# Scoring for the row maxima half a head group further ahead, six transfers of K and Q pieces a group, and a new prologue order, in a three-layer decoder kernel

## The chip, the cores and the metric

The kernel runs on one core of one Trainium2 chip. The metric is the device time of one launch in microseconds. Engines are named as in the profile: PE (matmuls), PEld (its weight loads), DVE, ACT, POOL, and SP, which here only issues DMAs.

## What is computed

Four sequences (B = 4) of 512 tokens of width 256 pass three layers, each with a residual and a LayerNorm behind it. Cut to what matters:

```python
# 1: recurrence with a gate, then an MLP
x_norm = layernorm(x) * g1 + b1
c_r, c_i = chunked_eigenstate(sigmoid(log_decay), frequency, x_norm @ w_in.T)   # 64 modes, chunks of 64
x1 = x + sigmoid(x_norm @ w_gate.T + b_gate) * (mix(c_r, c_i) @ w_out.T)
x = layernorm(x + x1 + silu(layernorm(x1) @ w_mlp1.T + b) @ w_mlp2.T + b2)
# 2: causal attention, 16 heads of 16, K and V from a second input
Q, K, V = x @ wq.T + bq, ctx @ wk.T + bk, ctx @ wv.T + bv
x = layernorm(x + softmax(causal(Q @ K.T / 4)) @ V @ wo.T + bo)
# 3: 48 experts, each takes its 64 best tokens; scatter-add of the weighted results
x = layernorm(x + experts(x))
```

## The kernel before

All five engines have a program of their own, written out by hand; they meet only in semaphores, and each engine takes its instructions strictly in the order of its own list. PSUM has eight banks of 512 float32.

**First layer** (to about 204 us). The batches are overlapped: while the MLP of batch b runs (`expand`, L1442, and `shrink`, L1451), the recurrence of batch b+1 goes through DVE and POOL. At the very start there is nothing to overlap. DVE builds the phases of the rotation first (14 chained instructions, L852 to L858, for the sine and for the cosine), and only then `ln_in(0)`: statistics (L824, L828), the root on POOL (L648, L650), the normalization (L837). ACT makes sine, cosine and then copies the transposed tokens out of PSUM with gain and bias (`turned_1`, L1207). PE transposes (L1397), projects (`project`, L1413 and L1420), mixes (L1430); for the second batch it takes `turn`, `turn_2(0)`, `project(1)`, in that order, and then the loop starts with `expand(0)`.

**Attention** (to about 530 us). The 16 heads of a batch go in four groups of four. For float32 accuracy K and Q are each split into three bfloat16 pieces. A score is contracted over 96 rows, six blocks of 16: K's pieces stand in them in the order 0, 1, 2, 0, 1, 0 and Q's in the order 0, 0, 0, 1, 1, 2. Three further rows (99 in all) carry minus the row maximum in Q, in three pieces, against ones in K. The pieces are computed feature by feature, stored to DRAM (`pieces`, L523 and L525) and fetched back per group into the right partitions (`group_in`, L537): 12 transfers of 16 partitions x 4 heads x 512 tokens, 64 KB, in runs of 1 KB.

For every group there are two passes over the scores:

- the **score pass** (`scores`, L1563 adds the causal mask, L1567 the product) writes query-major scores into two PSUM banks in turn, 11 banks a group, and DVE takes each bank's row maxima (`maxima`, L991). When all 11 are there, DVE negates and splits them (`negate`, L1002 to L1009), PE transposes them into the two spare banks (`minus_max`, L1579), and ACT copies them into Q's three extra rows (L1279);
- the **shifted pass** (`shifted`, L1597) computes key-major scores that already have the maximum subtracted, ACT takes the exponentials (L1292), POOL masks the diagonal (L711), and PE multiplies with V (`values`, L1610).

A group has four slots (b, g, j), one for each tile j of 128 keys. Lists called `PREPARE` (K, Q, V of the next batch), `ENTER` and `FINISH` (the output projection, LayerNorm and router logits of the batch that is done) say which further steps go into which slot; each engine works through the three step lists of a slot in order, between its shares of the score pass. The score pass of the *next* group (`then`) is spread over the slots: slot 0 has tiles 0 and 1 (three banks), slot 1 tile 2 (four), slot 2 tile 3 (four, all in the middle share), slot 3 none. `negate` closes slot 2 on DVE and `minus_max` stands in slot 3 on PE and ACT. The steps and `minus_max` and `heads_out` share the two spare banks (`take`): a step waits until the one before it in its bank has been read.

SP's list in a batch (`relay`) is: wait for and store K's and Q's pieces (`split_out`), fetch group 0 of the next batch, fetch the tokens, fetch groups 1 to 3, each behind the shifted pass that frees its place, fetch the context, store the outputs.

Before the first slot, the last MLP runs out; SP fetches all four groups; PE scores group 0, DVE takes its maxima; DVE normalizes the last batch; POOL computes that norm's root and *then* sets the ones in K (L723, four memsets), for which the first shifted pass waits.

**Experts** (to the end). After the top-64 selection on DVE (about 550 to 585 us) the weights of 24 pairs of experts stream through seven buffers.

## Time and profile before

| | us |
|---|---|
| median of three runs | 815.03 (811.88 to 816.0) |
| the profiled execution | 816.48 |
| its span | 814.7 |
| PE busy | 612.5 (75%) |
| DVE busy | 358.4 (44%) |
| ACT busy | 274.5 (34%) |
| POOL busy | 195.1 (24%) |

The page's second part divides the span into 40 slices of 20.4 us: PE's digits are 9 in slices 3 to 10 (the first layer), 7 and 8 through attention, and fall to 0 where the tokens are chosen; the DMA digit is 9 in the slices of the experts. The chain that ended last is PE 49%, DMA 16%, DVE 15%, issue 9%, ACT 7%. Busy shares are means over these unlike stages, so a reader should go to the stage: the PE's list in order of time shows for each instruction how long PE was idle ahead of it, and for whom.

### The profile page before, as it was taken

What the parts mean: (1) busy time and instruction counts of PE and PEld (TensorE: products, weight loads), DVE (VectorE), ACT (ScalarE), POOL (GpSimd) and SP (SyncE); (2) the same over time, 40 slices, a digit from 0 to 9 for tenths busy, and PEclk for the clock granted to TensorE, in tenths of its full rate; (3) what the DMA queues carried; (4) which work ended last, traced back from release to release, by engine and by line L of the source; (5) the groups of instructions that cost most, each with busy time, mean ns of one, the idle gap of its engine ahead of it and who ended that gap; (6) DMA issues with size and microseconds to landing.
All of it is one profiled execution on the core that took longest, in us unless ns stands there. A gap on an engine that the chain in (4) does not pass through costs nothing.

```text
span 814.7 us, 12126 instructions
## 1 busy us (share of the span) xinstructions
PE 612.5 (75%) x3942; PEld 351.0 (43%) x3942; DVE 358.4 (44%) x777; ACT 274.5 (34%) x458; POOL 195.1 (24%) x253
## 2 busy tenths in 40 slices
PE   3599999999467877787778788760089979789930
PEld 2458585847133445344534454340035535445520
DVE  3633533322564555455635564329823323223315
ACT  2141514141025463546354636510033322223304
POOL 1242221210051211021102111200032233335324
PEclk9899999999569899989998989965589999898965
DMA  6840000003410341134113334018159999994247
GB/s 229 299 162 1 0 0 0 25 27 108 138 40 1 113 140 45 40 116 135 38 46 114 109 114 179 1 53 338 84 176 372 408 387 326 315 378 88 35 98 231
DMA packets 53618, 112.25 MB, mean 138 GB/s; under 512 B 5920, under 2 KB 44496, under 8 KB 50512
## 3 DMA queue, kind: packets, MB, share of 16 engines
q1 hardware_dynamic: 48272, 105.06, 35.8%
q0 software_dynamic: 4608, 6.29, 4.1%
q10 hardware_dynamic: 704, 0.47, 0.2%
q8 instruction: 18, 0.29, 0.1%
q14 instruction: 16, 0.13, 0.1%
HBM read 91.88 MB, written 17.83 MB: 135 GB/s over the span
## 4 chain that ended last, share of the span: by engine, by line
PE 49%; DMA 16%; DVE 15%; issue 9%; ACT 7%; POOL 3%; SPq 1%; ACTq 0%; DVEq 0%; POOLq 0%
DMA sums<-row 9%; PE PS L1451 7%; PE PS L1442 7%; DMA sums<-wo_s,row 4%; DVE Mx L991 4%; PE PS L1730 4%; PE PS L1526 4%; PE PS L1610 3%; PE PS L1597 3%; PE PS L1567 3%; PE PS L1518 2%; PE PS L1413 2%; PE PS L1430 2%; PE PS L1563 2%; PE PS L1545 2%
## 5 line engine op out<-in xcount | busy, mean ns | idle before, releaser
L991 DVE TENSOR_REDUCE Mx<-PS 128x1 f32<-128x384 f32 (+3 forms) x176 | 107.3, 638 | 85.4 <-PE PS L1567 83.7
L1292 ACT ACTIVATE arena<-PS 128x512 f32<-128x512 f32 (+1 forms) x176 | 86.0, 565 | 87.6 <-PE PS L1597 87.6
L711 POOL TENSOR_SCALAR_AFFINE_SELECT arena<-arena 128x512 f32<-128x512 f32 x64 | 40.8, 638 | 217.9 <-ACT arena L1292 217.9
L1597 PE MATMUL PS<-arena 99*128 99x512 bf16 (+3 forms) x256 | 55.8, 307 | 26.3 <-ACT arena L1279 12.6
L1563 PE MATMUL PS<-causal,identb 128*128 128x128 bf16 (+2 forms) x176 | 45.8, 260 | 34.0 <-DVE Mx L991 24.7
L1567 PE MATMUL PS<-arena 96*128 96x128 bf16 (+3 forms) x256 | 68.1, 322 | 0.0
L1147 DVE TENSOR_TENSOR X<-PS,Y 128x512 f32<-128x512 f32 x48 | 31.4, 688 | 66.7 <-PE PS L1743 66.4
L1442 PE MATMUL PS<-arena 128*128 128x512 f32 x128 | 55.8, 593 | 1.6 <-issue 1.6
L1451 PE MATMUL PS<-arena 128*128 128x256 f32 x256 | 55.9, 379 | 0.0
L1359 ACT ACTIVATE X<-X 128x512 f32<-128x512 f32 x48 | 29.6, 632 | 71.3 <-DVE X L1147 68.1
L1610 PE MATMUL PS<-arena 128*32 128x128 f32 (+3 forms) x512 | 52.3, 481 | 1.0 <-POOL arena L711 0.9
L1451 PEld LDWEIGHTS PS<-arena 128*128 128x128 f32 x256 | 48.6, 190 | 6.6
L1563 PEld LDWEIGHTS PS<-causal,identb 128*128 128x128 bf16 x176 | 17.3, 98 | 72.5 <-DVE Mx L991 55.5
L1730 PE MATMUL PS<-ring_a,X 128*64 128x512 f32 x192 | 47.0, 635 | 0.5 <-ACT X L1348 0.5
L1597 PEld LDWEIGHTS PS<-arena 99*128 99x128 bf16 x256 | 21.2, 98 | 59.6 <-issue 17.5
L648 POOL TENSOR_SCALAR ve<-mv 128x4 f32<-128x4 f32 x16 | 3.7, 230 | 176.5 <-DVE mv L828 176.5
L1140 DVE COPY X<-PS 128x512 f32<-128x512 f32 x24 | 16.6, 692 | 66.1 <-PE PS L1730 66.1
L1730 PE MATMUL PS<-arena,X 128*64 128x512 f32 x192 | 44.6, 607 | 0.0
L1279 ACT ACTIVATE arena<-PS 3x1024 bf16<-3x1024 bf16 x32 | 30.8, 1009 | 40.3 <-PE PS L1579 40.2
L769 POOL DMA_INDIRECT sums<-row x16 | 25.6, 1597 | 64.6 <-issue 43.8
L1442 PEld LDWEIGHTS PS<-arena 128*128 128x128 f32 x128 | 24.2, 190 | 30.6 <-issue 30.0
L1207 ACT ACTIVATE arena<-PS,vec 128x512 f32<-128x512 f32 x16 | 11.4, 775 | 71.7 <-PE PS L1397 71.7
(183 smaller groups left out, 997.6 us busy)
## 6 DMA issues: line engine op xcount, KB each, us to landing
ring_a<-experts SPq DMA_DIRECT2D x12, 2048.0 KB, 10.2
arena<-experts SPq DMA_DIRECT2D x12, 2048.0 KB, 10.3
arena<-pieces SPq DMA_DIRECT2D x192, 64.0 KB, 2.3
ring_a<-experts SPq DMA_DIRECT2D x12, 512.0 KB, 4.8
arena<-experts SPq DMA_DIRECT2D x12, 512.0 KB, 7.4
pieces<-arena SPq DMA_DIRECT2D x4, 768.0 KB, 3.7
pieces<-ring_a SPq DMA_DIRECT2D x4, 768.0 KB, 3.7
X<-x SPq DMA_DIRECT2D x4, 512.0 KB, 3.6
```

Of the source, the lines that this page charges most:

```text
L711: pool.affine_select(out=pb[j % 2][:, :, 0:P], in_=pb[j % 2][:, :, 0:P], compare_op=ALU.is_ge, fill=0.0, base=0, pattern=[[0, GH], [1, P]] ...
L991: dve.tensor_reduce(Mx[:, g % 2, i, heads[0]:heads[-1] + 1], bank((g * NSH + u) % 2)[:, 0:len(heads) * w] .rearrange("p (h n) -> p h n", h ...
L1147: dve.tensor_tensor(hb[:, a * 512:(a + 1) * 512].rearrange("p (c n) -> p c n", c=8), bank(3 + a).rearrange("p (c n) -> p c n", c=8), b1_s[ ...
L1292: act.activation(pb[j % 2][:, heads[0]:heads[-1] + 1, 0:w], bank(2 + n % 3)[:, 0:len(heads) * w] .rearrange("p (h n) -> p h n", h=len(heads)),
L1442: mm = pe.matmul(bank(HIDDEN[m % 4]), wm1_s[:, k, m * P:(m + 1) * P], xT2[:, k, :], start=(k == 0), stop=(k == KT - 1))
L1451: mm = pe.matmul(PS[:, 6 * 512 + t * D:6 * 512 + (t + 1) * D], hid[:, m, t * P:(t + 1) * P], wm2_s[:, m, :], start=(m == 0), stop=(m == MT ...
L1526: mm = pe.matmul(o, w[:, k, :], xt[:, k, :], start=(k == 0), stop=(k == KT - 1))
L1563: pe.matmul(o[:, 0:len(heads) * w].rearrange("p (h n) -> p h n", h=len(heads)) [:, :, i * P:w], identb[:], wide(causal[:], len(heads)), st ...
L1567: mm = pe.matmul(o[:, a * w:(a + 1) * w], QTs[0:SK, g * GH + h, i * P:(i + 1) * P], KTs[0:SK, g * GH + h, 0:w], start=False, stop=True, sk ...
L1597: mm = pe.matmul(bank(2 + n % 3)[:, a * w:(a + 1) * w], KTs[0:SX, g * GH + h, j * P:(j + 1) * P], QTs[0:SX, g * GH + h, j * P:T], start=Tr ...
L1610: mm = pe.matmul(bank(6)[VW * h:VW * (h + 1), j * P:T], Vb[:, j, g * GH + h, :], pb[j % 2][:, h, 0:T - j * P], start=(j == 0), stop=(j == ...
L1730: mm = pe.matmul(bank(1 + n)[CAP * e:CAP * (e + 1), :], xgT[:, k, CAP * e:CAP * (e + 1)], w1_of[u][:, e, k, n * 512:(n + 1) * 512], start= ...
```

## The change

It does these things:

1. `SCORED`, `TILE_ORDER`, `AHEAD`: the tiles are scored in the order 3, 2, 0, 1. Slots 2 and 3 of group g score tiles 3 and 2 of group g+2; slot 0 of the next group scores tiles 0 and 1 of the same one, slot 1 none. `negate` moves to slot 0 on DVE, `minus_max` to slot 1 on PE and ACT.
2. `PREPARE`: K's projection moves from slot 1 to slot 0 of group 1, the query's input to slots 0 and 1, Q's last piece from slot 3 to slot 2; V's first half goes to the third list of its slot.
3. `group_in`: six transfers a group in place of twelve, of 3, 2 and 1 pieces' rows for K and the same for Q. The features inside a half of 128 are reordered on the host (`by_part`), so that the four heads of a group lie side by side: runs of 4 KB in place of 1 KB. A source is piece x feature x (head, token); where the same piece is wanted several times, its outermost step is zero.
4. The first shifted banks wait for the first of the two copies only.
5. Attention's start: the ones are set ahead of the last norm's root; after group 0, eight banks of group 1 are scored ahead of the first slot, and DVE takes the statistics of the last norm between the two.
6. The start of the kernel: DVE's statistics come ahead of the phases, its normalization ahead of them too; PE takes `project(1)` ahead of `turn_2(0)`.

```diff
-K_PIECES = (0, 1, 2, 0, 1, 0)
-Q_PIECES = (0, 0, 0, 1, 1, 2)
-NRD = 2 * NPR
+K_RUNS = ((0, 1, 3), (0, 1, 2), (0, 1, 1))
+Q_RUNS = ((0, 0, 3), (1, 0, 2), (2, 0, 1))
+NRD = len(K_RUNS) + len(Q_RUNS)
...
-TILES_OF = [(0, 1), (2,), (3,), ()]
-CUTS = [(2, 3), (2, 3), (0, 4), (0, 0)]
+TILE_ORDER = (3, 2, 0, 1)
+STARTS = [sum(len(SHARED_Q[t]) for t in TILE_ORDER[:n]) for n in range(TT)]
+SCORED = {i: list(zip([i] * NSH, range(start, NSH), SHARED_Q[i]))
+          for i, start in zip(TILE_ORDER, STARTS)}
+
+
+
+TILES_OF = [(0, 1), (), (3,), (2,)]
+AHEAD = (1, 1, 2, 2)
+CUTS = [(3, 3), (0, 0), (2, 3), (2, 3)]
 
 
 def _cut(tiles, cuts):
-    banks = [(i, n, heads) for i in tiles
-             for n, heads in enumerate(SHARED_Q[i], sum(len(q) for q in SHARED_Q[:i]))]
+    banks = [bank for i in tiles for bank in SCORED[i]]
     return banks[:cuts[0]], banks[cuts[0]:cuts[1]], banks[cuts[1]:]
 
 
-SCORED = [_cut(tiles, cuts) for tiles, cuts in zip(TILES_OF, CUTS)]
+SHARES = [_cut(tiles, cuts) for tiles, cuts in zip(TILES_OF, CUTS)]
 
 
 
 
 PREPARE = {
-    (1, 0): ([("query_in", 0)], [], [("query_in", 1)]),
-    (1, 1): ([("key", 0)], [("key", 1)], [("query", 0)]),
-    (1, 2): ([("split_k", 0)], [("query", 1)], []),
-    (1, 3): ([("split_q", 0)], [], []),
-    (2, 1): ([], [("value", 0)], []),
+    (1, 0): ([("key", 0)], [("key", 1)], [("query_in", 0)]),
+    (1, 1): ([("query_in", 1)], [("split_k", 0)], [("query", 0)]),
+    (1, 2): ([("query", 1)], [], [("split_q", 0)]),
+    (2, 1): ([], [], [("value", 0)]),
...
+                ahead = [None] + [(c, g + n) if g + n < NG else (c + 1, g + n - NG)
+                                  for n in (1, 2)]
+                for n in (1, 2):
+                    if last and g + n >= NG:
+                        ahead[n] = None
...
+                    do(c, g, j, prev, ahead[1], ahead[AHEAD[j]], *steps)
...
-                rows_g = slice(GH * HD * (g % 2), GH * HD * (g % 2) + GH * HD)
-                for n, (dst, order) in enumerate(((KTs, K_PIECES), (QTs, Q_PIECES))):
-                    for r, c in enumerate(order):
-                        sp.dma_start(dst[HD * r:HD * r + HD, heads, :],
-                                     pieces[n, c, g // 2, rows_g, :]
-                                     .rearrange("(h d) t -> d h t", d=HD)).then_inc(kq_in[g].s, 16)
+                at = GH * (g % 2)
+                for n, (dst, runs) in enumerate(((KTs, K_RUNS), (QTs, Q_RUNS))):
+                    first = 0
+                    for c, step, count in runs:
+                        part = pieces[n, c:c + (count if step else 1), g // 2]\
+                            .rearrange("c (d h) t -> c d h t", d=HD)[:, :, at:at + GH, :]\
+                            .rearrange("c d h t -> c d (h t)")
+                        if not step:
+                            part = part.to_broadcast([count, HD, GH * T])
+                        sp.dma_start(dst[first:first + HD * count, heads, :]
+                                     .rearrange("p h t -> p (h t)"), part).then_inc(kq_in[g].s, 16)
+                        first += HD * count
...
+            pool.wait_ge(vset, 2)
+            pool.wait_ge(m2.s, m2.now(B - 1, 1))
+            for g in range(NG):
+                pool.memset(KTs[SK:SX, GH * g:GH * g + GH, :], 1.0).then_inc(ones, 1)
+            pool.wait_ge(ones, NG)
...
+            dve.wait_ge(x_in.s, x_in.now(0, 1))
+            statistics(ln1, X, 0, 0, 0)
...
+            norm(ln1, rs1, X, lambda t: xn1[:, t, :], 0, 0, (xt1.s, xt1.before(0, 1)))
+            phase(0.0, rot[:, 0:C])
+            phase(0.25, rot[:, C:2 * C])
...
-            def dve_slot(b, g, j, prev, then, *steps):
-                shares = SCORED[j] if then is not None else ([], [], [])
-                maxima(then, shares[0])
+            def dve_slot(b, g, j, prev, then, scored, *steps):
+                shares = SHARES[j] if scored is not None else ([], [], [])
+                maxima(scored, shares[0])
                 if j == 0 and prev is not None:
                     divide(*prev)
                 dve_do(steps[0])
-                maxima(then, shares[1])
+                maxima(scored, shares[1])
                 dve_do(steps[1])
-                maxima(then, shares[2])
-                if j == 2 and then is not None:
+                maxima(scored, shares[2])
+                if j == 0 and then is not None:
...
+            for i in TILE_ORDER:
+                maxima((0, 0), SCORED[i])
             negate(0, 0)
-            ln_out_norm(B - 1)
+            dve.wait_ge(ln3.s, ln3.now(B - 1, 1))
+            statistics(ln3, X, (B - 1) * TT, B - 1, 1)
+            for i in TILE_ORDER[:2]:
+                maxima((0, 1), SCORED[i])
+            norm(ln3, rs3, X, lambda t: X[:, (B - 1) * TT + t, :], (B - 1) * TT, B - 1)
...
-                if j == TT - 1 and then is not None:
+                if j == 1 and then is not None:
...
             turn(ln1, xt1, xn1, 1, 4, (xe1.s, xe1.now(0, KT)))
+            project(1)
             turn_2(0)
-            project(1)
...
-                if j == 0:
-                    pe.wait_ge(nte.s, nte.now(b, 2 * g + 2))
                 for n, heads in enumerate(SHARED[j], FIRST[j]):
+                    if j == 0 and heads[0] % 2 == 0:
+                        pe.wait_ge(nte.s, nte.now(b, 2 * g + heads[0] // 2 + 1))
...
-            def pe_slot(b, g, j, prev, then, *steps):
-                shares = SCORED[j] if then is not None else ([], [], [])
+            def pe_slot(b, g, j, prev, then, scored, *steps):
+                shares = SHARES[j] if scored is not None else ([], [], [])
                 for n, _ in enumerate(shifted(b, g, j)):
                     of = len(SHARED[j])
-                    scores(then, shares[0][n * len(shares[0]) // of:
...
             minus_max(0, 0)
+            for i in TILE_ORDER[:2]:
+                scores((0, 1), SCORED[i])
...
+    by_part = lambda m: m.reshape(KT, 2 * GH, HD, -1).swapaxes(1, 2).reshape(m.shape)
...
+        "w_q": by_part(w("xattn_wq_w")).T,
+        "w_kv": np.concatenate([by_part(w("xattn_wk_w")), w("xattn_wv_w")]).T,
...
```

## Rows read from the trace of the kernel before

**Rows 1.** Busy time by stretch: each engine's busy us, PE clock, DMA share, GB/s.

```profile
209.70:530.00 320.30, 248.10 (x1812) 132.18 (x1812) 170.22 (x372) 151.30 (x264) 62.74 (x80) 0.90 0.26 84
...
611.00:652.00 41.00, 41.00 (x366) 20.67 (x362) 14.24 (x24) 13.43 (x25) 12.13 (x16) 1.00 1.01 390
```

**Rows 2.** PE's waits in attention, 250 to 530 us: total, times, longest.

```profile
PE PS L1563 <- DVE Mx L991: 23.4, 25, 3.6
PE PS L1597 <- ACT arena L1279: 11.3, 11, 1.3
```

**Rows 3.** PE in order of time: where each group's shifted pass starts.

```profile
329.33 0.60 PE L1597 MATMUL PS<-arena 99*128 99x512 bf16 x2
...
356.94 0.61 PE L1597 MATMUL PS<-arena 99*128 99x512 bf16 x2 [1.35 <-ACT arena L1279]
...
371.65 0.61 PE L1597 MATMUL PS<-arena 99*128 99x512 bf16 x2 [0.92 <-ACT arena L1279]
...
384.67 0.60 PE L1597 MATMUL PS<-arena 99*128 99x512 bf16 x2 [0.92 <-ACT arena L1279]
...
411.16 0.61 PE L1597 MATMUL PS<-arena 99*128 99x512 bf16 x2
```

**Rows 4.** PE in order of time, inside group 1.

```profile
340.42 1.88 PE L1526 MATMUL PS<-arena,wq_s 128*128 128x512 f32 x4
...
346.86 0.29 PE L1563 MATMUL PS<-causal,identb 128*128 128x128 bf16 x1 [3.57 <-DVE Mx L991]
...
347.97 3.62 PE L1526 MATMUL PS<-arena,wq_s 128*128 128x512 f32 x4
```

**Rows 5.** DVE in order of time: Q's last piece, then group 3.

```profile
354.97 1.23 DVE L966 TENSOR_TENSOR ring_a<-ring_a 128x1024 bf16<-128x1024 f32 x1 [1.13 <-ACT ring_a L1268]
...
372.74 1.47 DVE L991 TENSOR_REDUCE Mx<-PS 128x4 f32<-128x512 f32 x2 [3.77 <-PE PS L1567]
...
378.43 2.52 DVE L991 TENSOR_REDUCE Mx<-PS 128x1 f32<-128x512 f32 x4 [0.16 <-PE PS L1567]
...
381.73 0.18 DVE L1009 TENSOR_TENSOR nst<-Mr,nst 128x16 bf16<-128x16 f32 x1
```

**Rows 6.** ACT in order of time: the shift rows' copies in group 3.

```profile
382.69 1.93 ACT L1279 ACTIVATE arena<-PS 3x1024 bf16<-3x1024 bf16 x2 [0.72 <-PE PS L1579]
```

**Rows 7.** SP's issues: at attention's start, then in a batch.

```profile
202.16 22.79 SPq L537 DMA_DIRECT2D arena<-pieces  x48
...
356.22 0.37 SPq L525 DMA_DIRECT2D pieces<-ring_a  x1
360.11 5.48 SPq L537 DMA_DIRECT2D arena<-pieces  x12
```

**Rows 8.** DMA issues by line: count, KB each, median us to landing.

```profile
arena<-pieces SPq DMA_DIRECT2D x192, 64.0 KB, 2.3
```

**Rows 9.** All engines in order of time, attention's start.

```profile
219.62 1.86 PE L1579 MATMUL PS<-identb,nst 128*3 128x128 bf16 x16 [1.65 <-DVE nst L1009]
...
223.30 7.55 POOL L723 MEMSET arena<- 3x2048 bf16 x4 [0.32 <-POOL rstd L650]
...
230.90 1.04 PE L1597 MATMUL PS<-arena 99*128 99x512 bf16 x2 [9.41 <-POOL arena L723]
```

**Rows 10.** All engines in order of time, the kernel's start.

```profile
8.34 1.40 DVE L824 BATCH_NORM_STATS2 stats<-X 128x6 f32<-128x256 f32 x4 [0.17 <-DVE arena L858]
...
14.41 1.45 ACT L1207 ACTIVATE arena<-PS,vec 128x512 f32<-128x512 f32 x2 [5.96 <-PE PS L1397]
...
33.51 1.45 ACT L1207 ACTIVATE arena<-PS,vec 128x512 f32<-128x512 f32 x2 [6.76 <-PE PS L1397]
```

**Rows 11.** The chain that ended last, the kernel's start: start, us, what.

```profile
41.37 3.95 PE PS L1413 x8
45.32 3.45 PE PS L1420 x16
48.77 13.73 PE PS L1442 x32
```

32 lines of the change are left out of this document (10 added, 22 removed).

## The prediction

> **What bounds the kernel now.** I read the times by stage first, then PE's waits, then PE, DVE, ACT and the DMA queue in order of time over one batch of attention. Three stages follow each other. To 204 us the matmuls of the first block fill PE apart from its first 49 us; from 570 us the experts stream, with the DMA engines full [rows 1]; neither end is touched. Between them, from 209.7 to 530, lies attention, where PE is busy 248.1 of 320.3 us [rows 1], idle for over a fifth. Its two longest waits there are for row maxima of DVE, 23.4 us in 25 waits, and for the shift rows that ACT copies into Q, 11.3 us in 11 [rows 2]. A batch goes through four head groups, whose shifted pass starts at 329.33 (group 1), 356.94 (group 2), 371.65 (group 3), 384.67 (group 0 of the next batch) and 411.16 [rows 3]: 27.6 + 14.7 + 13.0 + 26.5 = 81.8 us. Group 3 does nothing but attention; group 1 also projects K and Q of the next batch, group 2 half of V, group 0 finishes the old batch.
>
> In group 3 the last maximum ends at 378.43 + 2.52 = 380.95. Then negation, transposes and copies follow, and the next shifted pass starts at 384.67 [rows 3, 5, 6]: 3.7 us in which DVE and most of PE hang on one chain. That chain is what the change takes off.
>
> **Part 1: scores half a group further ahead.** No instruction is added in a group; 11 banks of scores and 11 maxima stay. Slot 0 now holds three banks, slot 1 none, slots 2 and 3 four each. The plain group in its new order: DVE's first two maxima end at 1.1 + 1.4 = 2.5 us after the group's start [rows 3, 5], the third at 3.2, division 0.7 and negation 0.9 reach 4.8. PE finished the passes of slot 1 near 3.5, so it waits some 1.4 us in front of the transposes, a wait that the change adds, with the first value matmuls queued behind it. Transposes 0.7 and values 1.0 end at 6.6. Then come eight banks, bound by DVE: four of 0.63 [rows 5] and four of 0.56 (estimate from the same row, three quarters of the width and a fixed part) are 4.8, with 0.8 for the first fill and the last values. Sum 12.2 where it was 13.0. The shift chain is hidden under slots 1 to 3, but the maxima now bunch where PE has least else to do: **0.8 us a group**, not 3.7. Group 2 the same with its half of V: 14.0.
>
> Group 1: before, four banks stood behind DVE's last piece of K, a stall of 3.57 us, and the next Q projection then ran at the lower clock, 3.62 instead of 1.88 [rows 4]. Both go (K's pieces are prepared in slots 0 and 1, where no maxima are queued behind). Against that, ACT's second exponentials stand behind the K pieces, and the transposes' second bank waits for the query copy: 1.4 back. 27.6 - 3.6 - 1.7 - 0.8 + 1.4 = 22.9. The last piece of Q (1.23 us on DVE [rows 5]) is then done some 20.8 us into the group, against 26.9 before [rows 3, 5].
>
> Group 0: the transposes now stand between the two output projections and share their two spare PSUM banks. The first needs output 0 read by DVE (0.9), the second output needs both copies of ACT out of the bank, 1.93 us [rows 6]: +2.9. At its end the four further maxima and the normalization stand in front of the last values, and eat the 0.8 of the plain group and 0.2 more. 26.5 + 3.1 = 29.6. A batch: 22.9 + 14.0 + 12.2 + 29.6 = 78.7, **3.1 less, 9.3 in the three full batches**. In the last batch group 1 gains 0.8; group 2 scores only three banks and needs about 6.6 + 2.4 = 9.0 (4.0 less): -4.8. Bounds: my walk of the two loaded groups may be off by 2 us each; a batch gains from -1 (loses 1) to 6 us.
>
> **Part 2: prologue.** The statistics go ahead of the 14 phase steps on DVE. Before, the phase steps end and the statistics start at 8.34, and ACT evacuates the first transposes at 14.41 [rows 10]. Now the statistics start with the input, near 4.8 (estimate: the steps started near 4.9, each 0.23, and I assume the input no later), norm and root end near 9.6, the steps near 12.9, and ACT, whose order is unchanged, is held by the cosine to 13.2: -1.2. Projection 1 (3.95 + 3.45 us) stood behind the transposes of the second norm, from 41.37, though its input left ACT at 33.51 + 1.45 = 34.96 [rows 10, 11]. Placed ahead it ends near 41.3, the transposes and ACT's copy end at 44.1 where the hidden layer started at 48.77: -4.5 with the 1.2. PE is then busy without a break, so all of it should reach the end. Bounds -3 to -5.5.
>
> **Part 3: the ones and the priming.** The memsets, 7.55 us on POOL, end at 230.9, and PE waited 9.41 us for them [rows 9]. They move behind the MLP's last matmul at 202.2 and run beside the transfers of the first group: nothing is left of them; the root on POOL behind them is not late, since its statistics come after 217. What is late next: eight more banks of the second group are scored first, 8 x 0.63 = 5.0, and DVE's statistics, 2.0, stand ahead of their maxima. Scoring group 0 and its negation took from the landing at about 209.7 to the transposes at 219.62 [rows 8, 9], 9.9 us. The start therefore hangs on when the pieces land, which is part 4.
>
> **Part 4: six transfers a group.** Before, 48 issues take 22.79 us, 0.475 each, and one of 64 KB lands 2.3 us after its issue [rows 7, 8]: group 0 after 11 x 0.475 + 2.3 = 7.5. Now a group is 3, 2 and 1 rows of pieces, twice, in runs of 4 KB instead of 1 KB. No row shows such a transfer; every one of before has 16 or more rows as the outermost dimension of both sides, the new sources have 3 or 2 (the pieces). Lower bound: spread over all 16 engines, a group lands in 5 x 0.475 + 2.3 = 4.7 us. Upper bound: cut along the outermost dimension only, a transfer of 192 KB uses three engines and one of 128 KB two, 64 KB each, and two engines carry all four large ones: 4 x 65.5 KB = 262 KB. A full engine moves 390 / 16 / 1.01 = 24.1 GB/s [rows 1]: 10.9 us, with 2.3 some 13.2. I take the upper end: the two sides share no larger outer factor by which a splitter could cut them, and the issue order puts nothing on the other 13 engines.
>
> The Trainium skill weighs in here with two rules that pull apart. "DMA: Bandwidth & Descriptors", section "Rules for kernel authors", says to gather many small transfers into a large one, which would give the 4.7 us. Its section "Why a DMA increments its semaphore by 16 and not by 1" says that the number of engines is the largest up to 16 that divides the slowest dimension of both sides, which gives 3 and 2 and the 13.2 us; the trace of before, whose outermost dimensions are multiples of 16, shows neither.
>
> With 13.2: group 0 lands at 215.4, group 1 at 226.3; transposes 225.3 to 227.2, eight banks, shifted pass near 232.4: 1.5 later than 230.9 [rows 9]. In the batches, Q leaves at 20.8, its store takes 3.9 (356.22 to 360.11 [rows 7]), the group lands at 24.7 + 13.2 = 37.9 after the start of group 1. It is wanted in slot 2 of group 2, at 22.9 + 8.6 = 31.5: **PE waits 6.2 to 6.4 us, three times, 18.8**. That is the place where the lead of half a group is given back: the scores ask for the pieces half a group sooner, and the transfer is the late one. With 4.7 they land at 29.4, in time. The later groups have six slots of room either way.
>
> **Sum** for the profiled run, 816.5 (span 814.7 and 1.8 around it, 1.5 above the median of 815.03): -4.5 (prologue) +1.5 (start) -0.9 (first group, no ones wait behind it) -9.3 -4.8 +18.8 = +0.8. So 817.3, less 1.5 for the median: **816**. Own range 806 to 822 (batch gain 1 to 5, engine rate up to a fifth higher).
>
> **Rivals.** (a) The transfers spread over all engines: -4.5 -7.0 (the start at 223.9) -0.9 -9.3 -4.8 = -26.5, 789; with its bounds 780 to 797. For it: the 1 KB transfers of before do spread, and larger runs are moved faster. (b) They spread, but the walk of the slots is wrong and the bunched maxima and shared banks leave nothing of the 9.3: 799. (c) Slower: the three waits of over 6 us let TensorE's clock fall. In rows 4 a wait of 3.57 us was followed by work at half rate, the lower level, costing 1.7 us in one projection and about 2.5 in all that followed to the next group; here the score banks, values and half of V behind a wait of 6 cost some 2.5 each time, 7.5, and 824. It decides from a wait as long as that 3.57; what speaks against it is that in slots 2 and 3 PE waits for DVE anyway, so a slower PE is partly hidden. (d) The change does not lead: if Q's last piece comes as late as before, 26.9 into the group, even a spread transfer lands at 35.5, and 4 us a batch are lost on (a): 801; held with (b).
>
> **Chances.** Forecast 0.45, (a) 0.27, (b) and (d) 0.10, (c) 0.18. About 0.5% is what a measurement of this kernel can tell from no change. Faster by more: all of (a), most of (b) and (d), and a quarter of the forecast's range: 0.27 + 0.09 + 0.12 = 0.48. Slower: (c) and a fifth of the forecast, 0.18 + 0.10 = 0.28. Rest 0.24. The range, 784 to 824, leaves out the fast end of (a) and the slow end of (c).
>
> **What would show it.** Right: PE waits for pieces in slot 2 of each group 2, several us, and the transfers of 192 KB land 4 us or more after issue, the last of six over 10; the ones leave the chain; a hidden layer that starts near 44. Wrong, if the first score of the batch waits for no transfer (then a); if group 0 takes 26 us or less, part 1's bank sharing is mis-sized; if a plain group is under 11.5 us, the bunching is hidden.

## The result, and the profile after

The changed kernel takes 836.25 us (median; 833.22 to 838.27) where the kernel before took 813.45 beside it: a ratio of 1.027, with a 95% interval from 1.023 to 1.031. It is **slower by some 22 us**. The prediction said 816, with a range up to 824: both the time and the range were wrong. The profiled execution took 834.7 us, its span 833.0, against 816.48 and 814.7 before.

The page after: span, busy times, shares of the chain that ended last, and the group of the first matmuls of a score bank (busy, mean ns | idle before them and what ended most of it).

```profile
span 833.0 us, 12063 instructions
...
PE 620.8 (75%) x3942; PEld 344.4 (41%) x3942; DVE 356.8 (43%) x777; ACT 274.8 (33%) x458; POOL 195.8 (24%) x253
...
PE 47%; DMA 21%; DVE 13%; issue 8%; ACT 6%; POOL 2%; SPq 1%; DVEq 0%; POOLq 0%; ACTq 0%
...
L1589 PE MATMUL PS<-causal,identb 128*128 128x128 bf16 (+2 forms) x176 | 47.4, 269 | 59.8 <-DMA arena<-pieces 33.7
```

The work of the engines is the same: as many matmuls and DVE operations as before. What has changed is what PE waits for. Its waits in attention, 205 to 545 us (total, times, longest), where [rows 2] stood before:

```profile
PE PS L1589 <- DMA arena<-pieces: 33.7, 4, 13.8
PE PS L1589 <- DVE Mx L1014: 25.0, 36, 2.6
PE PS L1605 <- DVE nst L1032: 6.7, 9, 1.6
PE PS L1623 <- ACT arena L1318: 6.1, 20, 0.6
```

The wait of the shifted pass for ACT's copies of the shift rows, 11.3 us before [rows 2], is gone: the lead does what it says. The wait for maxima has not shrunk: from 250 us on, as in [rows 2], it is 22.9 against 23.4 us, and from 205 us on 25.0 against 24.7. One for the pieces stands above all: once at the start of attention, once in each full batch. PE in order of time, over the start and one batch; the last column is the idle time before an instruction and what ended it:

```profile
212.11 0.26 PE L1589 MATMUL PS<-causal,identb 128*128 128x128 bf16 x1 [13.79 <-DMA arena<-pieces]
...
228.45 1.03 PE L1623 MATMUL PS<-arena 99*128 99x512 bf16 x2
...
242.91 0.61 PE L1623 MATMUL PS<-arena 99*128 99x512 bf16 x2
...
266.56 1.03 PE L1623 MATMUL PS<-arena 99*128 99x512 bf16 x2
...
282.62 0.28 PE L1589 MATMUL PS<-causal,identb 128*128 128x128 bf16 x1 [6.26 <-DMA arena<-pieces]
...
284.76 1.51 PE L1636 MATMUL PS<-arena 128*32 128x384 f32 x8
...
289.60 0.60 PE L1623 MATMUL PS<-arena 99*128 99x512 bf16 x2
...
301.81 0.60 PE L1623 MATMUL PS<-arena 99*128 99x512 bf16 x2
...
316.22 1.99 PE L1544 MATMUL PS<-wo_s,Y 128*128 128x256 f32 x8 [0.71 <-ACT arena L1305]
...
321.81 0.23 PE L1589 MATMUL PS<-causal,identb 128*128 128x128 bf16 x1 [2.60 <-DVE Mx L1014]
...
326.39 0.23 PE L1589 MATMUL PS<-causal,identb 128*128 128x128 bf16 x1 [1.79 <-DVE Mx L1014]
...
328.29 1.97 PE L1531 MATMUL PS<-ident,ring_a 128*128 128x128 f32 x8
330.95 3.57 PE L1665 MATMUL PS<-arena,wr_s 128*64 128x512 f32 x4 [0.69 <-ACT arena L1277]
334.45 0.60 PE L1623 MATMUL PS<-arena 99*128 99x512 bf16 x2
```

The shifted passes that open groups 1, 2, 3 and 0 stand at 242.91, 266.56, 289.60 and 301.81, the next batch at 334.45: groups of 23.7, 23.0, 12.2 and 32.6 us, together 91.5, where rows 3 gave 27.6, 14.7, 13.0 and 26.5. The same subtraction for the other kernels gives this table, which the rest goes by. It holds the mean over the three full batches; the first three lines are before, what was predicted of after, and after.

| us | group 1 | group 2 | group 3 | group 0 | batch |
|---|---|---|---|---|---|
| before | 27.3 | 14.7 | 13.0 | 26.6 | 81.7 |
| predicted of after | 22.9 | 20.3 (6.3 of it wait) | 12.2 | 29.6 | 85.0 |
| after | 23.3 | 22.8 (6.6 of it wait) | 12.2 | 32.2 | 90.5 |
| six_spread | 23.3 | 15.7 | 12.2 | 32.9 | 84.1 |
| twelve_rows | 23.3 | 15.6 | 12.2 | 32.6 | 83.7 |
| late_copies | 23.3 | 15.6 | 12.2 | 32.8 | 83.9 |
| spread_early_norm | 23.7 | 16.2 | 12.2 | 29.3 | 81.3 |
| late_copies_early_norm | 22.9 | 15.2 | 12.2 | 26.0 | 76.3 |
| old_slots | 26.2 | 14.7 | 12.9 | 27.2 | 81.1 |
| old_slots_early_norm | 26.1 | 14.7 | 12.9 | 29.8 | 83.5 |
| confined_busy | 23.7 | 21.4 | 12.2 | 31.4 | 88.6 |
| confined_early_norm | 23.3 | 23.1 | 12.2 | 30.7 | 89.3 |
| before_six_confined | 26.8 | 14.7 | 16.8 | 26.4 | 84.7 |

SP's issues at the start of attention and in a batch show the transfers (start, us, count), to be read against [rows 7]:

```profile
198.35 32.25 SPq L553 DMA_DIRECT2D arena<-pieces  x24
...
268.11 3.79 SPq L553 DMA_DIRECT2D arena<-pieces  x6
...
273.48 29.46 SPq L553 DMA_DIRECT2D arena<-pieces  x18
```

At the start PE goes on at 212.11, 13.8 us after the first issue (198.35), in the batch 14.5 after it (268.11 to 282.62); the prediction said 13.2. And half as many issues as before take longer to issue: 24 in 32.25 us where 48 took 22.79. In three stretches in which PE waits for pieces (busy us of each engine, PE clock, share of the 16 DMA engines, GB/s):

```profile
199.00:211.00 12.00, 0.00 (x0) 0.00 (x0) 0.65 (x1) 0.00 (x0) 6.49 (x4) 0.59 0.26 83
276.00:282.00 6.00, 0.36 (x4) 0.08 (x1) 0.88 (x4) 0.60 (x1) 0.00 (x0) 0.81 0.25 86
366.00:373.00 7.00, 0.00 (x0) 0.00 (x0) 0.41 (x3) 0.25 (x1) 0.00 (x0) 0.67 0.28 89
```

All wait for data, and the DMA engines are busy for a quarter of their time on average: the transfers go over few of them, as the next experiment shows by contrast. When a single one of these transfers lands, the page of after doesn't say (compare [rows 8], which have a landing time behind the KB):

```profile
arena<-pieces SPq DMA_DIRECT2D x32, 192.0 KB
```

### The profile page after: what moved, and what is told of

It is laid out like the page before. It is cut to its first block, busy times and chain, and to the rows that moved or that the text cites. A ratio compares the mean times of both kernels' runs of the same rounds, so it can differ in the third digit from the quotient of the medians.

```text
span 833.0 us, 12063 instructions
## 1 busy us (share of the span) xinstructions
PE 620.8 (75%) x3942; PEld 344.4 (41%) x3942; DVE 356.8 (43%) x777; ACT 274.8 (33%) x458; POOL 195.8 (24%) x253
## 4 chain that ended last, share of the span: by engine, by line
PE 47%; DMA 21%; DVE 13%; issue 8%; ACT 6%; POOL 2%; SPq 1%; DVEq 0%; POOLq 0%; ACTq 0%
DMA sums<-row 7%; PE PS L1468 7%; PE PS L1477 7%; DMA arena<-pieces 5%; DMA sums<-wo_s,row 4%; PE PS L1757 4%; PE PS L1636 4%; DVE Mx L1014 3%; PE PS L1593 3%; PE PS L1552 2%; PE PS L1544 2%; DMA wkv_s<-x_rows,row 2%; PE PS L1439 2%; PE PS L1623 2%; PE PS L1589 2%
## 5 line engine op out<-in xcount | busy, mean ns | idle before, releaser
L1014 DVE TENSOR_REDUCE Mx<-PS 128x1 f32<-128x512 f32 (+3 forms) x176 | 106.9, 638 | 94.9 <-PE PS L1593 94.1
L1593 PE MATMUL PS<-arena 96*128 96x512 bf16 (+3 forms) x256 | 72.1, 337 | 0.0
L1623 PE MATMUL PS<-arena 99*128 99x512 bf16 (+3 forms) x256 | 59.7, 316 | 6.2 <-ACT arena L1318 6.1
L1173 DVE TENSOR_TENSOR X<-PS,Y 128x512 f32<-128x512 f32 x48 | 31.4, 687 | 66.9 <-PE PS L1770 66.5
L1636 PE MATMUL PS<-arena 128*32 128x128 f32 (+3 forms) x512 | 54.9, 484 | 2.0 <-POOL arena L732 1.9
L1233 ACT ACTIVATE arena<-PS,vec 128x512 f32<-128x512 f32 x16 | 11.3, 774 | 67.3 <-PE PS L1423 67.3
## 6 DMA issues: line engine op xcount, KB each, us to landing
arena<-experts SPq DMA_DIRECT2D x12, 512.0 KB, 11.3
```

What stands on the lines that cost most here:

```text
L1014: dve.tensor_reduce(Mx[:, g % 2, i, heads[0]:heads[-1] + 1], bank((g * NSH + u) % 2)[:, 0:len(heads) * w] .rearrange("p (h n) -> p h n", h ...
L1173: dve.tensor_tensor(hb[:, a * 512:(a + 1) * 512].rearrange("p (c n) -> p c n", c=8), bank(3 + a).rearrange("p (c n) -> p c n", c=8), b1_s[ ...
L1593: mm = pe.matmul(o[:, a * w:(a + 1) * w], QTs[0:SK, g * GH + h, i * P:(i + 1) * P], KTs[0:SK, g * GH + h, 0:w], start=False, stop=True, sk ...
L1623: mm = pe.matmul(bank(2 + n % 3)[:, a * w:(a + 1) * w], KTs[0:SX, g * GH + h, j * P:(j + 1) * P], QTs[0:SX, g * GH + h, j * P:T], start=Tr ...
L1636: mm = pe.matmul(bank(6)[VW * h:VW * (h + 1), j * P:T], Vb[:, j, g * GH + h, :], pb[j % 2][:, h, 0:T - j * P], start=(j == 0), stop=(j == ...
```

## The experiments

Twelve kernels ran. Durations of groups are taken from the traces, the verdict from the ratio to the kernel before in the same comparison. Spans are compared with care, for two reasons. First, kernels with the same first 40 us reach attention at different times: the first issue of pieces stands at 198.35 in after, 195.74 in six_spread and 194.01 in confined_busy. It comes from PE's clock at the kernel's start: the first projection, the same eight matmuls, takes 6.42, 5.37 and 3.67 us in them, and the mixing behind it 5.20, 3.69 and 3.69; the two together make these differences to within 0.1 us. Second, what follows the start of the last group's shifted pass, mostly the experts, takes 295.0 us in before, 296.0 in after and 296.1 in six_spread, but between 285.6 (spread_early_norm) and 299.7 (before_six_confined) in the profiled executions of the others. The group durations carry neither.

### Undo the confinement: six_spread

Only the order of dimensions on the DRAM side changes: the 16 features stand outermost, the 3 or 2 pieces behind them. Same bytes, same six transfers, same runs of 4 KB.

```diff
-    .rearrange("c (d h) t -> c d h t", d=HD)[:, :, at:at + GH, :]
-    .rearrange("c d h t -> c d (h t)")
+    .rearrange("c (d h) t -> d c h t", d=HD)[:, :, at:at + GH, :]
+    .rearrange("d c h t -> d c (h t)")
-    part = part.to_broadcast([count, HD, GH * T])
+    part = part.to_broadcast([HD, count, GH * T])
```

> The changed kernel with one thing other: the six transfers name the feature (16) as the outermost dimension of their source and the piece (3 or 2) inside it, so both sides begin with a multiple of 16. Theory 1 (the transfers ran on three and two engines, and all that the prediction missed hangs on that, the clock behind the waits included): the waits for pieces, 33.7 us in 4 in the changed kernel, fall to some 5 (one, at the start); group 2 takes 14.0 us where it took 23.0, the start is 9 us earlier, in all 9 + 3 x 9 = 36 less: about 800. Theory 2 (the order of the slots is at fault, shared spare banks and bunched maxima): the waits go, but group 0 stays at 32.6 us; if nothing of the clock comes back, about 806; before stays the better if it is over 815. If a spread transfer were no faster: no change, 836.

Measured: 801.2 us, a ratio of 0.985 [0.978, 0.992]; the profiled span is 805.1. PE's longest total wait, SP's issues at the start, and the landing times by the page:

```profile
PE PS L1589 <- DVE Mx L1014: 25.0, 34, 2.6
...
195.74 14.81 SPq L553 DMA_DIRECT2D arena<-pieces  x24
...
arena<-pieces SPq DMA_DIRECT2D x32, 192.0 KB, 3.5
arena<-pieces SPq DMA_DIRECT2D x32, 128.0 KB, 3.4
```

The share of the DMA engines while PE waits at the start of attention, and what they moved, in the same columns as above:

```profile
196.00:202.00 6.00, 0.00 (x0) 0.00 (x0) 1.04 (x1) 0.00 (x0) 6.00 (x4) 0.79 0.74 171
```

They are busy for 0.74 of their time and move 171 GB/s, where after had 0.26 and 83. The 24 issues take 14.81 us instead of 32.25, 192 KB land 3.5 us after issue, and the waits in the batches are gone but for 0.5 us in one of them (group 2: 15.7 against 22.8). So the confinement, not the size of the transfers, is what cost: by the spans 27.9 us, of which 2.6 are the kernel's start (198.35 against 195.74), so 25.3; by the ratios 4.2% or some 34, with half-widths of 0.4 and 0.7%. (The profiled execution of six_spread, 806.79 us, was the slowest of its four, so the spans give the low end.) But the batches take 84.1 us, where the prediction gave them 78.7 once nothing waits for pieces. The same miss as in after, without the transfers: its cause lies elsewhere.

### Many rows or few transfers: twelve_rows

Twelve transfers of one piece instead of six, with the new runs of 4 KB; all have 16 rows outermost.

```diff
-K_RUNS = ((0, 1, 3), (0, 1, 2), (0, 1, 1))
-Q_RUNS = ((0, 0, 3), (1, 0, 2), (2, 0, 1))
+K_RUNS = tuple((c, 1, 1) for c in (0, 1, 2, 0, 1, 0))
+Q_RUNS = tuple((c, 1, 1) for c in (0, 0, 0, 1, 1, 2))
```

> The changed kernel with twelve transfers a group, of 16 partitions each, in runs of 4 KB. Theory 1: spread over 16 engines, each 64 KB; 12 issues of some 0.45 us and 2.3 to land are 7.5 us a group, 2.8 more than six spread ones; at the start that is 2.8 us, in the batches the pieces are just late (24.7 + 7.5 = 32.2 against 31.5 wanted), so some 3 to 5 us above six_spread: about 804. If the count of issues and not the spread was what mattered, it would be as slow as the changed kernel or slower, 836 and more.

Measured: 802.51 us, 0.988 [0.980, 0.996]; batches of 83.4, 82.0 and 85.7 us, and no wait for pieces in a batch.

```profile
arena<-pieces SPq DMA_DIRECT2D x192, 64.0 KB, 2.3
```

64 KB still land after 2.3 us, as they did in runs of 1 KB [rows 8]. Once all are spread, six transfers and twelve are the same within the intervals: gathering them is worth nothing that can be measured here; what counts is that they are spread.

### The confined transfers alone: before_six_confined

The kernel before with the six transfers of the change and the row order of the weights that they need (by_part), nothing else.

```diff
+            .rearrange("c (d h) t -> c d h t", d=HD)[:, :, at:at + GH, :]
+            .rearrange("c d h t -> c d (h t)")
...
-        "w_q": w("xattn_wq_w").T,
+        "w_q": by_part(w("xattn_wq_w")).T,
```

> The kernel before with nothing but the six transfers as the change writes them (and the order of features they need). Theory 1: the start is some 6 us later (group 0 lands 13.7 us after the last matmul of the MLP instead of 7.6); in the batches group 0 of the next batch has the pieces 13.4 us after SP begins where it had 7.8, and 4 us of slack: 2 us of waiting three times. In all +10 to +14: about 825. Theory 2 (transfers are not to blame): 813.

Measured: 833.94 us, 1.024 [1.015, 1.033]; the first shifted pass at 237.06 instead of 230.90, and the batches 84.7 instead of 81.7.

```profile
PE PS L1569 <- DMA arena<-pieces: 22.3, 4, 14.0
```

The direction was expected, the size missed by some 9 us. In the old order, too, the pieces come late: group 3, where the next batch's scores begin, takes 16.2, 15.6 and 18.6 us instead of 13.0. Half a group less of lead helps only in part (8.3 us of such waits in the batches, 19.9 in after). Of the 20.7 us between the spans 6.2 lie ahead of the first shifted pass, 0.7 in the first group and 9.2 in the batches; the other 4.7 lie behind the last group, where nothing was edited.

### Two gains alone: before_prologue, before_ones

The kernel before with the new order of the prologue (statistics and norm ahead of the phase steps, projection 1 ahead of the second norm's transposes), and the kernel before with the memsets of the ones behind the MLP's last matmul.

```diff
+            statistics(ln1, X, 0, 0, 0)
             dve.wait_ge(consts, CONSTS)
...
-            turn_2(0)
             project(1)
+            turn_2(0)
```

> The kernel before with the new order of the first 50 us alone (statistics and norm ahead of the phases on DVE, the second projection ahead of the second transposes on PE). The prediction said -4.5; in the changed kernel the last matmul of the MLP ended 3.8 us earlier. Expected -3.8, about 809.6, since nothing behind it depends on the time of day. If the gain is given back at the start of attention: 813.

Measured: 809.11 us, 0.992 [0.988, 0.997].

```diff
+            for g in range(NG):
+                pool.memset(KTs[SK:SX, GH * g:GH * g + GH, :], 1.0).then_inc(ones, 1)
+            pool.wait_ge(ones, NG)
             root(ln3, rs3, B - 1, 1 + 2 * TT)
```

> The kernel before with the four memsets of ones moved ahead of the last norm's root on POOL, nothing else. The wait of 9.41 us goes; next are the copies of the shift rows, done at 222.6 in the profile of before where the first shifted matmul stood at 230.9: -8.2 at most. DVE's normalization then stands ahead of the first maxima, and POOL's bias ahead of the first mask: I expect 6 to 8 less, about 806.5. If the memsets are hidden by something as long: 813.

Measured: 804.83 us, 0.990 [0.986, 0.994]. The first shifted pass stands at 223.44 in place of 230.90 [rows 9]. Both gains are there alone, 0.8 and 1.0%, with half-widths of 0.4%. Expected were 3.8 us (0.5%) and 6 to 8 us (0.7 to 1.0%), so both sizes lie within what was measured.

### Is the lead worth anything: old_slots

six_spread, so with prologue, early ones and spread transfers, but with the old order of the slots and no scores of group 1 ahead of the first slot.

```diff
-TILES_OF = [(0, 1), (), (3,), (2,)]
-AHEAD = (1, 1, 2, 2)
-CUTS = [(3, 3), (0, 0), (2, 3), (2, 3)]
+TILES_OF = [(0, 1), (2,), (3,), ()]
+AHEAD = (1, 1, 1, 1)
+CUTS = [(2, 3), (2, 3), (0, 4), (0, 0)]
```

> Spread transfers, new prologue, ones set early, but the slots as in the kernel before (scores of the next group alone, negation in slot 2, transposes and copies in slot 3, K and Q prepared as before, nothing scored ahead of group 0). Theory A (the new order of the slots costs: in the run with spread transfers a batch takes 80.9 to 85.7 us where it took 81.8, and its lead pays only at the two ends): a batch is back at 81.8, which gives some 7 us over the three; the start keeps the early ones and early pieces; the last two groups lose 4. In all 2 to 4 us below the spread run: about 798. Theory B (the lead of half a group is a gain of its own in the batches, as the prediction had it, 3.1 each): 801 + 9 + 4 - 5 = 809.

Measured: 804.16 us, 0.987 [0.980, 0.994], between the two expectations, and not to be told from six_spread (0.985). The traces show why. In six_spread the three batches take 9 us more (252.3 against 243.3); its first group takes 14.8 us instead of 20.7, and its last batch, from the start of group 1 to that of group 3, 22.6 instead of 25.5. 9.0 - 5.9 - 2.9 = 0.2: the lead gives at the ends what it takes in the loop. In the loop group 1 gains 2.9 and group 3 0.7, group 2 loses 1.0 and **group 0 5.6**.

### What group 0 loses: late_copies, spread_early_norm, late_copies_early_norm

Group 0 of six_spread, first full batch, PE and DVE in order of time:

```profile
298.12 1.99 PE L1544 MATMUL PS<-wo_s,Y 128*128 128x256 f32 x8 [0.71 <-ACT arena L1305]
...
303.71 0.23 PE L1589 MATMUL PS<-causal,identb 128*128 128x128 bf16 x1 [2.60 <-DVE Mx L1014]
...
305.96 1.69 DVE L854 TENSOR_SCALAR ring_a<-ring_a,mv,rstd 128x256 f32<-128x256 f32 x4
...
310.85 1.72 PE L1531 MATMUL PS<-ident,ring_a 128*128 128x128 f32 x8
...
313.26 1.93 PE L1665 MATMUL PS<-arena,wr_s 128*64 128x512 f32 x4 [0.69 <-ACT arena L1277]
315.12 0.60 PE L1623 MATMUL PS<-arena 99*128 99x512 bf16 x2
```

Two suspects. The second output projection (298.12) waits for ACT's copies out of the bank that it shares with the transposes. And the normalization (305.96) stands behind four maxima, and the transposes of its result (310.85) and the router's logits (313.26) stand last in the group, behind every value matmul.

**late_copies** moves the transposes and copies in group 0 behind the second output projection:

```diff
-                if j == 1 and then is not None:
+                if j == (2 if g == 0 else 1) and then is not None:
                     minus_max(*then)
```

> Spread transfers, new slots, with one step moved: in group 0 of each batch the transposes of the negated maxima and their copies come in slot 2 and not in slot 1, so that they no longer stand between the two output projections in the shared spare banks. The prediction priced that sharing at 2.9 us in each of three group 0. Expected: group 0 falls from 31.4 to 33.7 to some 28.5 to 30.5, 3 x 2.9 = 8.7 less, 793; where TensorE's clock stays up in the logits because of it, 2 more each. If the sharing is hidden behind DVE's chain of output, statistics and maxima: no change, 801.

Measured: 804.16 us, 0.990 [0.982, 0.998]; group 0 32.8 us: no gain.

```profile
308.95 0.23 PE L1589 MATMUL PS<-causal,identb 128*128 128x128 bf16 x1 [1.68 <-DVE Mx L1014]
...
310.75 1.97 PE L1531 MATMUL PS<-ident,ring_a 128*128 128x128 f32 x8
313.40 3.67 PE L1665 MATMUL PS<-arena,wr_s 128*64 128x512 f32 x4 [0.69 <-ACT arena L1277]
```

The second output starts 2.8 us sooner in its group. By PE's wait for the maxima behind the normalization (1.68 us here) only 0.8 to 1.2 us of that are left, in all three batches: the transposes that go with the copies now lie between the score banks of slot 2, and PE runs part of that slot at the lower clock. The rest goes at the group's end: the logits take 3.67 us in all three batches, at half the rate, where six_spread has 1.93, 3.67 and 3.56.

**spread_early_norm** leaves the copies as in six_spread, and puts the normalization ahead of slot 2's maxima and the transposes of its result ahead of slot 3's score banks:

```diff
-    (0, 2): ([], [], [("norm", 0)]),
-    (0, 3): ([], [], [("turn", 0), ("turn", 1), ("logits", 0)]),
+    (0, 2): ([("norm", 0)], [], []),
+    (0, 3): ([("turn", 0), ("turn", 1)], [], [("logits", 0)]),
```

> Spread transfers and new slots; in group 0 the normalization after two of the eight maxima and the transposes of its result ahead of the last score banks, but the shift rows' copies left in slot 1. With the copies late as well it took 783.7, with the copies late alone 804.2. If what closes group 0 is the norm behind four maxima and PE's list behind it, the copies matter little: 784 to 787. If the two output projections still wait for each other over the spare banks (2.9 in each group 0, seen as 17.2 against 20.0 us from the group's start to the wait for the maxima) and nothing eats that now: 792.

Measured: 795.25 us, 0.978 [0.973, 0.984]; group 0 29.3 us instead of 32.9. That is above both expectations, but nearer to the second: the output projections still wait for each other, and it costs. PE's wait of 1.46 to 1.68 us for the maxima behind the norm is gone in all three batches, and the logits take 1.93 us in all three.

**late_copies_early_norm** has both edits:

> As the run with the late copies, and in group 0 the normalization comes after two of the eight bunched maxima instead of four, and PE's transposes of its result stand ahead of the last two score banks instead of behind all values. Expected, if the chain statistics, maxima, normalization, transposes, logits closes group 0: 1.5 to 3 us less a batch than with the late copies alone, about 787; if PE's order merely moves the same waits: no change against it.

Measured: **783.74 us, 0.962 [0.956, 0.968]**: faster than before by some 31 us, and some 52 under the median of after. Group 0 takes 26.0 us, a batch 76.3. PE and DVE in the same group as above:

```profile
295.46 1.99 PE L1544 MATMUL PS<-wo_s,Y 128*128 128x256 f32 x8
...
301.99 1.69 DVE L854 TENSOR_SCALAR ring_a<-ring_a,mv,rstd 128x256 f32<-128x256 f32 x4 [0.40 <-POOL rstd L666]
...
305.90 1.04 PE L1531 MATMUL PS<-ident,ring_a 128*128 128x128 f32 x8
...
308.34 1.93 PE L1665 MATMUL PS<-arena,wr_s 128*64 128x512 f32 x4
310.20 0.61 PE L1623 MATMUL PS<-arena 99*128 99x512 bf16 x2
```

The second output no longer waits, and starts 2.8 us sooner in its group, which begins at 283.90 here and at 283.72 in six_spread. The normalization stands behind two maxima, its transposes lie among score banks, and the logits wait for nothing: from the start of the transposes PE needs 4.3 us to the next shifted pass in both, but now two score banks and the last two sets of values lie in between. The two causes are not additive: the late copies give nothing alone and 3.3 us a group on top of the early norm (29.3 to 26.0), which alone gives 3.6.

### The same edit where the lead or the spread is missing: old_slots_early_norm, confined_early_norm

The FINISH edit of spread_early_norm, once in old_slots and once in after.

> Spread transfers, prologue and ones as changed, slots as before, with the norm ahead of the four maxima of slot 2 and the transposes ahead of the last values. If the early norm is a gain by itself: 804 - 9 or more, 795 or less. If it pays only where negation does not close the group (in the old order the maxima behind the norm hold the negation, the transposes and the copies of the next group, so 1.7 us of norm stand on that chain): 802 to 807.

Measured: 806.02 us, 0.990 [0.984, 0.995]; group 0 goes from 27.2 to 29.8 us. In the old order the edit brings nothing and costs in group 0: the place of the norm is wrong only once the maxima are bunched by the lead. What it costs there is on DVE:

```profile
309.61 1.69 DVE L855 TENSOR_SCALAR ring_a<-ring_a,mv,rstd 128x256 f32<-128x256 f32 x4 [1.58 <-POOL rstd L667]
```

DVE waits 1.58 us for POOL's root and then normalizes, ahead of the four maxima that the negation needs, so the negation ends 24.0 us into the group instead of 20.4, and the next shifted pass hangs on it.

> The changed kernel as it is, its transfers on three and two engines, with the early norm alone. If the two causes add (36 for the transfers, some 17 for the norm's place): 836 - 17 = 819. If the shorter group 0 only lets PE reach the wait for pieces sooner (the pieces are asked for by steps of group 1, so they move with it): still 819. If the transfers then also delay the context or group 3: above 825.

Measured: 828.13 us, 1.019 [1.012, 1.025], 8 us under after; group 0 from 32.2 to 30.7, and the waits for pieces stay (group 2 23.1). The expectation of 819 took 17 us for the norm's place, and on that it missed. The same edit gives 6 us of median and 8.3 in the batches when it goes from six_spread to spread_early_norm, and 8 us of median, but only 3.5 in the batches, here. So the edit helps with and without the waits for pieces: what group 0 loses and what the pieces cost are two causes. Whether they add exactly these runs don't show.

### What the clock costs behind a wait: confined_busy

after, with 26 matmuls added where PE waits for the batch's pieces, into a score bank that the next score overwrites. They do nothing for the result; they keep PE at work.

```diff
+                    if u == 0 and g == 0 and not isinstance(b, int):
+                        pe.wait_ge(mxs.s, mxs.before(b, NSH * NG + u - 1))
+                        for _ in range(26):
+                            pe.matmul(bank(0).rearrange("p (h n) -> p h n", h=4), identb[:],
+                                      wide(causal[:], 4), start=True, stop=True, ...)
```

> The changed kernel, transfers confined, with 26 added matmuls of 128x512 bf16 (0.22 us each at the higher clock, 5.7 us) in the bank that is free, put where PE waits for the pieces in slot 2 of each group 2, so that PE is at work during that wait of 5.7 to 8.0 us. It computes the same. If the clock that falls in these waits costs what rival (c) said (2.5 us each): the rows behind the wait (values of tile 1, 1.51 us at the lower level) return to 0.85, and the time falls by 4 to 7, to about 830. If the clock is given back elsewhere, or the waits for the maxima, not those for the pieces, set it: 836 within 2. If the added work outlasts the wait: above 836.

Measured: 826.32 us, 1.011 [1.005, 1.017]: more work, and some 10 us less than after. PE where after showed a wait of 6.26 us and values of 1.51:

```profile
275.02 5.78 PE L1584 MATMUL PS<-causal,identb 128*128 128x512 bf16 x26
280.63 0.22 PE L1595 MATMUL PS<-causal,identb 128*128 128x128 bf16 x1
...
282.23 0.85 PE L1642 MATMUL PS<-arena 128*32 128x384 f32 x8
```

The pieces are there when the 26 end, the values take 0.85 us. Batches of 88.6 us, three times, where after has 91.5, 91.4 and 88.5: 5.6 us less in all, 4.3 of it in group 2 and 2.5 in group 0, and 1.2 back in group 1. That is within the 4 to 7 us expected. The effect is clearest behind the wait: from the batch's first score to the end of group 2 PE takes 6.98, 7.38 and 6.73 us in after and 5.7 each time here, 4.1 us in all. The other 2.4 of the 8.0 us between the spans lie outside the batches: the kernel's start is 4.3 us earlier here, by a first projection of 3.67 us and not by the edit, and 2.7 are given back until the end of the first group, with 0.8 less behind the last one. The difference of the ratios, 1.6% with half-widths of 0.4 and 0.6%, says 13 us, more than the traces of one execution each show; part of it can be the start. What the clock costs here is therefore some 4 to 6 us by the traces and more by the ratios, and known no better.

## Why the prediction was wrong, and where it was right

The profiled executions, by the steps of the sum:

| us | predicted | measured |
|---|---|---|
| prologue (first issue of pieces 198.35, before 202.16) | -4.5 | -3.8 |
| from there to the first shifted pass (30.1, before 28.7) | +1.5 | +1.4 |
| first group (14.5, before 17.4) | -0.9 | -3.0 |
| three waits for pieces (6.26, 7.97, 5.67) | +18.8 | +19.9 |
| three batches without these waits | -9.3 | **+6.6** |
| last batch (22.6, before 26.4) | -4.8 | -3.8 |
| the rest | 0 | +1.0 |
| sum | +0.8 | +18.3 |

**Right: the transfers.** That six large transfers would be slower than twelve small ones was the step with least cover in the trace of before, and it held: 13.8 us to the first score against 13.2, three waits of 19.9 us in all against 18.8, in the slot and the group that were named, with 0.25 to 0.28 of the DMA engines busy. The Trainium skill, page "DMA: Bandwidth & Descriptors", section "Why a DMA increments its semaphore by 16 and not by 1", says that the number of engines is the largest up to 16 that divides the slowest dimension of both sides; six_spread, where 3 or 2 became 16 there, bears it out, with a DMA share of 0.74 in place of 0.26, 192 KB in 3.5 us and 25.3 us of span won. The forecast's own price of the confinement was 18.8 and 8.5 at the start, 27.3; between after and six_spread the batches give 19.1 and the way from the first issue to the first shifted pass 6.4. What no step had: SP itself is held back, with 24 issues over 32.25 us. The prediction also said that every transfer of before has 16 or more rows outermost; the 24 biases of 2 KB have 2, and the page gives no landing time for them, as it gives none for the new transfers. So its sign "192 KB land 4 us or more after issue" stays unread; the first score, 13.8 us after the first issue, stands for it.

**Right: prologue, ones, plain group.** Group 3 takes 12.2 us, as walked slot by slot. The prologue gave 3.8 of 4.5: ACT evacuates the first transposes at 13.02 (14.41 before [rows 10], 13.2 predicted) and the hidden layer starts at 44.70 (48.77 [rows 11], 44.1 predicted). But the first projection behind it ran largely at the lower clock and took 6.42 us, where before had 4.80 (the mixing took 5.20 and 5.38); that varies from one execution to the next and is no part of the change. PE in after, the two first projections, the mixing, and the projections of the second batch, in order of time:

```profile
14.71 6.42 PE L1439 MATMUL PS<-arena 128*128 128x512 f32 x8 [2.26 <-ACT arena L1233]
20.97 3.62 PE L1446 MATMUL PS<-arena 128*128 128x256 f32 x16
27.44 5.20 PE L1456 MATMUL PS<-arena 128*128 128x256 f32 x16 [2.85 <-POOL arena L675]
...
35.05 3.70 PE L1439 MATMUL PS<-arena 128*128 128x512 f32 x8 [1.54 <-ACT arena L1233]
38.58 3.62 PE L1446 MATMUL PS<-arena 128*128 128x256 f32 x16
```

**Wrong: the term of the batches.** "A batch: 22.9 + 14.0 + 12.2 + 29.6 = 78.7, 3.1 less" should have been 83.9 (90.5 less the wait of 6.6): a miss of 5.2 us a batch, 15.5 in all (15.9 against the 245.0 that the three batches of before really take), nearly the whole of the 17.5 by which the sum was off. Its bounds, from a loss of 1 to a gain of 6 us a batch, didn't hold it either. It went wrong in two places:

- *Group 0, 29.6 against 32.2.* The prediction had the bank sharing (2.9; the second output starts 2.8 sooner without it, and the group gives 3.3 once nothing eats that) and named the norm behind four maxima, but priced that at 1.0 us: "eat the 0.8 of the plain group and 0.2 more". With the norm moved, the group takes 3.6 us less in six_spread. Behind the norm stands a chain that nothing covers: transposes, ACT's copy, logits, the next shifted pass. The step counted DVE's time and not what PE has left to do beside it. Two things came on top: the maxima behind the norm make PE wait (1.79 us, at 326.39; 1.46 to 1.80 in the three batches of after and of six_spread), and around that wait part of PE's work runs at the lower clock, in one place or another: the logits took 3.57, 1.93 and 1.93 us in after and 1.93, 3.67 and 3.56 in six_spread, but between 1.93 and 2.11 in all nine batches of the kernels that have the early norm and the lead.
- *Group 2, 14.0 and 6.3 wait against 22.8.* The wait is 6.6. Without it, 16.2 are left; the fastest group 2 of six_spread takes 14.7, 0.7 more than walked. Of the other 1.5 the kept-busy PE of confined_busy gives back 1.4, all of it behind the first score (4.1 us in three batches): behind a wait of 6.26 us, in a stretch with a granted clock of 0.81, a mix of the two levels (1.2 and 2.4 GHz), values took 1.51 us that take 0.85 there.

**The rivals.** (c), the clock behind the three waits, was a real mechanism, priced at 7.5 us where the traces of confined_busy give 5.6 and the ratios speak for more. It should not have been a rival with a chance of 0.18 but a term of the forecast, since rows 4 show it behind a shorter wait. With it the sum would have been 824, still 12 under the median of after: the miss of group 0 and the clock come together, and the range ended where it had only one of them. (b), for spread transfers and nothing left of the 9.3, gave 799, and six_spread measured 801.2; in it the batches not only lose the 9.3 but take 7.3 us more than those of before, and the start and the end make up for that. (a), 789, is what the change would have given with the batches as walked; late_copies_early_norm shows that the lead is worth more than that, -16.1 us over three batches (228.9 against 245.0), but only with the end of group 0 in another order. (d) doesn't hold: group 1 takes 23.3 us, and SP issues the store of Q 21.3 us into it (264.25), where the walk said 20.8.

**What stays open.** Why group 2 takes 16.2 us in two of the three batches of six_spread, where no piece is waited for: PE already runs at the lower clock when it starts (0.66 us for the last values of group 1, where the first batch has 0.42), and what lowered it there was not tested. Why the first group gained 3.0 us where the sum had 0.9. How much of the difference between ratios and spans in confined_busy is the clock elsewhere in the kernel. And why the batches of after take 91.5, 91.4 and 88.5 us: the slow work behind the wait is there in the third too (6.73 us, values of 1.38), but its wait is shorter (5.67 us) and its group 0 takes 31.3 us instead of 32.6 and 32.7.

## What to carry to other kernels

Before transfers are gathered into fewer, look at the outermost dimension on both sides: six transfers, four of them with 3 or 2 rows outermost, cost 25 us of span here (some 34 by the ratios), and turning two dimensions on the DRAM side gave them back. A lead asks for its inputs sooner and bunches the work that it moves: check when they land, and place the chain that ends the group (norm, transposes, logits) ahead of the bunch, not behind it; that order, with the copies out of the shared bank behind the second output, decided here whether half a group of lead was worth nothing (0.985 against 0.987) or 2.5% (0.962). And price a stall of PE with the clock behind it, wherever a row shows slow work after a shorter one.

## What the runs showed of the hardware

- Few DMA engines hold the issuing queue back, too. The same 24 issues of the same bytes took 32.25 us on SP confined and 14.81 spread; the trace of after gives the times of single issues on that line, in ns, as the smallest, the median and the largest: 412, 658 and 4379.
- The length of a contiguous run (4 KB or 1 KB) and the number of transfers (24 or 48) made no difference that could be measured once all were spread: 2.3 us for 64 KB in both, 801.2 and 802.51 us.
- Work that does nothing can pay: 26 matmuls, 5.78 us, in a wait that lasts anyway, in each of three batches, took 5.6 us off the batches, 4.1 of them right behind the wait.
- The same eight matmuls at the kernel's start took between 3.67 and 6.48 us in executions of kernels that are alike up to there: a few us between two spans are no verdict on an edit behind them.
